# Expert results copied out of PSUM earlier in the next expert's second unit

## What is computed

```python
shared = jax.nn.silu(xt @ sw1) * (xt @ sw3) @ sw2
...
h = jax.nn.silu(jnp.einsum('td,edh->eth', xt, w1)) * jnp.einsum('td,edh->eth', xt, w3)
y = jnp.einsum('eth,ehd->etd', h, w2)
...
out = jnp.einsum('te,etd->td', comb, y) + shared
```

## Time and profile before

| what | value |
|---|---|
| median of 3 runs | 856.68 us (854.65 to 857.11) |
| the profiled execution | 855.59 us |
| its span in the trace | 854.0 us |
| granted TensorE clock, mean | 0.955 of full |
| TensorE busy | 767.4 us (90%) |
| VectorE busy | 554.9 us (65%) |
| ScalarE busy | 460.8 us (54%) |
| GpSimd busy | 301.0 us (35%) |

### The profile page before, as it was taken

One profiled execution on the slowest core, in us unless ns is written; L12 is line 12 of the kernel. 1 busy time (PEld: TensorE's weight loads), 2 busy tenths in 40 slices (PEclk: granted clock), 3 DMA queues, 4 the chain that ended last, 5 costly groups with the idle time before them and its releaser, 6 DMA issues. The chain is left out here.

```text
span 854.0 us, 13328 instructions
## 1 busy us (share of the span) xinstructions
PE 767.4 (90%) x4993; PEld 640.5 (75%) x4993; DVE 554.9 (65%) x904; ACT 460.8 (54%) x748; POOL 301.0 (35%) x189
## 2 busy tenths in 40 slices
PE   3997799999999978899996999799889899898894
PEld 2664588787878753899995999688788787786784
DVE  6628997979797926454226444478686786777755
ACT  4244596868686825633334332356565665566530
POOL 8240686868686820000000004033222222232333
PEclk9999799999999989899998699999999999999998
DMA  9320830000000006000004208756565766556015
GB/s 260 119 41 9 298 67 2 1 2 2 1 2 2 1 9 251 1 1 1 2 0 152 71 1 297 249 175 224 174 237 193 231 207 210 194 196 218 34 37 162
DMA packets 66460, 92.46 MB, mean 108 GB/s; under 512 B 6723, under 2 KB 44197, under 8 KB 65877
## 3 DMA queue, kind: packets, MB, share of 16 engines
q1 hardware_dynamic: 64149, 85.77, 30.9%
q0 software_dynamic: 2240, 5.76, 2.2%
HBM read 80.69 MB, written 10.82 MB: 107 GB/s over the span
## 5 line engine op out<-in xcount | busy, mean ns | idle before, releaser
L1581 POOL TENSOR_TENSOR w_lo<-weights_far,w_hi 128x1024 fp32r<-128x1024 f32 x32 | 77.0, 2406 | 210.9 <-ACT w_hi L1699 210.9
L660 POOL TENSOR_TENSOR bias_exp_hi<-edge_exp_hi,mask 128x640 fp32r<-128x640 f32 x40 | 98.0, 2451 | 71.3 <-PE ps L806 32.3
L1784 PE MATMUL ps<-xT,w_hi 128*128 128x480 f32 (+7 forms) x512 | 112.1, 342 | 3.6 <-DVE w_lo L1601 3.6
L1784 PEld LDWEIGHTS ps<-xT,w_hi 128*128 128x128 f32 x512 | 84.6, 194 | 9.9 <-issue 4.1
L1786 PEld LDWEIGHTS ps<-xT,w_lo 128*128 128x128 f32 x512 | 74.7, 192 | 1.7
L1786 PE MATMUL ps<-xT,w_lo 128*128 128x240 f32 (+7 forms) x512 | 75.4, 270 | 0.0
L806 PE MATMUL ps<-onehot,bias_exp_hi 128*128 128x314 f32 x400 | 69.5, 320 | 5.4 <-POOL bias_exp_hi L660 5.0
L1799 PE MATMUL ps<-w_hi,hidden_hi 128*128 128x512 f32 (+7 forms) x120 | 52.1, 434 | 23.0 <-DVE weights_near L1629 21.0
L1618 DVE TENSOR_TENSOR hT<-hT 128x240 f32<-128x240 f32 (+7 forms) x64 | 63.2, 988 | 11.3 <-ACT hT L1716 11.3
L1699 ACT ACTIVATE w_hi<-weights_far 128x1024 fp32r<-128x1024 f32 x64 | 67.1, 1050 | 0.0
L806 PE MATMUL ps<-onehot,bias_exp_lo 128*128 128x314 f32 x400 | 65.7, 311 | 0.0
(11 more groups left out here) (272 smaller groups left out, 1678.8 us busy)
## 6 DMA issues: line engine op xcount, KB each, us to landing
weights_far<-in_L_ffn_w SPq DMA_DIRECT2D x64, 512.0 KB, 5.5
weights_near<-in_L_ffn_w SPq DMA_DIRECT2D x32, 512.0 KB, 3.6
weights_near<-in_L_gnn_W SPq DMA_DIRECT2D x1, 4096.0 KB, 14.5
weights_near<-in_L_gnn_Wqkv SPq DMA_DIRECT2D x3, 1024.0 KB, 8.2
weights_ff<-in_L_gnn_W SPq DMA_DIRECT2D x1, 3072.0 KB, 13.9
weights_lo_shared<-in_L_ffn_sw SPq DMA_DIRECT2D x6, 512.0 KB, 7.7
weights_near<-in_L_ffn_sw SPq DMA_DIRECT2D x6, 512.0 KB, 6.7
slot_rows<-zeros SPq DMA_DIRECT2D x1, 2944.0 KB, 26.1
```

Of the source, the lines that this page charges most:

```text
L660: pool.tensor_tensor(to.rearrange("p t (h d) -> p t h d", h=H), e[:, b, :, :].unsqueeze(3).broadcast_to([P, CT, H, BN]), m.unsqueeze(2).br ...
L1581: pool.tensor_tensor(w2s[u][1], raw_rest[2] if v == V else raw[u][2], w2s[u][0], ALU.subtract)\
L1784: pe.matmul(both(bank, cap), w[u % 2][0][:, c, cut], xT(r)[:, c, :, :], start=c == 0, stop=False)
```

## The change

In VectorE's loop over the units, the call that copies the results of expert r - 1 is put between the first weight part of the unit and its first sum, instead of between the first product and the second sum. It is still in the second unit. Nothing else differs.

```diff
             for v in range(V):
                 r, u = v // UNITS, v % UNITS
                 weights_lo(v + 1, 0)
+                if u == 1 and r:
+                    results(r - 1)
                 parts_summed(v, 0)
                 weights_lo(v + 1, 1)
                 hidden(v, 0)
-                if u == 1 and r:
-                    results(r - 1)
                 parts_summed(v, 1)
                 if u == 2 and r + 1 < EX:
                     rows_lo(r + 1)
```

## The result

The changed kernel takes 844.69 us (median of 4 runs, 842.90 to 846.38), the kernel before beside it 856.89 us (854.65 to 857.95). The ratio is 0.9861, with a 95% interval of 0.9832 to 0.9889: 12.2 us faster, where 13.2 was forecast. The profiled execution has a span of 841.2 us, against 854.0.

A forecast was written before the change was run, and what follows sets the result against it. A dependency loop through ScalarE, VectorE and GpSimd sets the shortest unit, with TensorE late after pausing for copies. Savings of 13.9 us, less 0.1 per expert, give -13.2: 843.5 us for the median, range 841.0 to 850.0.

The forecast's parts named there:

- step 3: VectorE, second units: sum, GpSimd's pass and the held product come 1.20 us later behind the copies; seven times, 8.4 us.
- steps 1 and 2: TensorE's down-projection at 224: pause about 1.45 us instead of 3.42, then full clock, block 2.83 us instead of 4.39.
- t0: Start of a unit's first weight split on ScalarE, from which the forecast counts times within an expert.
- step 4: Third units: ScalarE's 3.23 us wait for TensorE goes, later waits too, and the unit reaches its shortest length.
- ring length: Shortest unit length, set by a dependency loop through ScalarE, VectorE and GpSimd: 7.85 us at capacity 224, then 7.75, 7.63.
- The sum: Whole program: the experts' savings together -13.9 us, less 0.1 per expert given back, so -13.2 us.
- the list: New and old lengths of experts by capacity, 224 to 128, second unit to next second unit; savings together -13.9 us.
- the allowance for the row splits: 0.1 us per expert given back, because the third unit also splits the next expert's rows.
- the first rival: TensorE's clock still falls behind the pauses: 0.6 us per expert, 4.2 in all, giving 847.7 us; chance 0.18.
- TensorE's new waits: TensorE's remaining waits for the copies: 1.45 us, then about 2.1, 2.4, 3.0; about 12 us in all, from 21.0.
- nothing: TensorE gains 8.7 us at its pauses, the 8.4 us price is paid in series: net -0.3, 856.4 us; chance 0.07.
- slower: Third unit's up-projections are held by something else, TensorE's early start is worth nothing: 8.4 us price, 865.1 us; chance 0.05.

The follow-up runs named there:

- two sizes of copies: Copies of experts 0 to 6 cut to 8 of 512 columns, in the changed kernel (ratio 0.9721) and in the kernel before (ratio 0.9920).
- short copies: The kernel before, with the copies of experts 0 to 6 cut to 8 of 512 columns: 852.89 us, ratio 0.9920.

## Why the prediction was right

**The step from 7.85 to 9.05 (step 3).** Right: 9.08, and +1.2 at every expert. The two sizes of copies showed that the price hangs on the place.

**The earlier start and the clock (steps 1 and 2).** Right at 224: a pause of 1.48 us for 1.45, a block of 2.86 for 2.83, the next up-projections 5.91 us after t0 (596.94 to 602.85) for 5.88 forecast. The step went from pause length to clock, and there it was too simple: the clock stayed full behind 2.27 and 2.64 us and fell behind 1.94 and 2.00.

**What it buys (step 4).** Right: ScalarE's wait fell from 25.0 to 0.6 us, and third units have ring length.

**The sum.** By expert, second unit to second unit (208, for instance, from 629.64 to 661.87): 32.70, 32.23, 31.64, 31.17, 31.31 and 30.21 us, where the list says 32.50, 32.08, 31.59, 31.08, 30.62 and 30.17. Five are within 0.2, the allowance for the row splits included in none of them. The sixth, capacity 160, is 0.7 long, and this is the first rival in small: behind the pause of 1.94 us the clock fell, and ScalarE then waited twice for TensorE, 0.27 and 0.30 us. The rival had put such a case at 0.6 us. It happened at one expert with consequences (at 128 the clock fell too, but TensorE has more room there), not at seven. The list alone comes to 13.9 us and the window shows 12.6. Of the 1.3 between them 0.7 is this one and 0.6 is spread over the others, about what the forecast gave back for the row splits (0.7). So what was off is the clock behind the pause at capacity 160, for which the sum had no term.

**TensorE's new waits.** 11.2 us for about 12; the one at 144 was 1.54 and not 2.4, as TensorE arrived later from the slow block before it (1.56 us more work in an expert that was 0.7 longer).

**The rivals "nothing" and "slower"** failed where the prediction said they would be decided. "Nothing" needed ScalarE's wait to stay, and it went. For "slower" the third unit's matmuls had to be held by a weight part; they started at 5.91 us after t0, right behind the block before them. The GPSIMD Engine Reference of the Trainium skill, Key points, says that GpSimd contends with Vector instructions that have two inputs in SBUF. The trace agrees: the product was held for 2.11 us beside the pass, and copies that no longer lie under the pass cost 1.2 us a time. That was not the whole sum.

What stays open is how the clock is decided. Pauses of equal length ended in either way (2.27 us: full in the second profile of the kernel before, low in the one with short copies), and no experiment here kept a pause and varied what TensorE does ahead of it.

## What to carry to other kernels

When an engine waits for an instruction that is ready long before its turn, ask what the turn costs in the place that it would move to: the same copies cost the unit 0 under another engine's pass, 1.2 us at the head of its ring, and almost 0 in a wait at the end of the unit before. Read a unit's shortest length off the units that nobody disturbs, and add to it; here that gave the time to 1.2 us. And when an engine's short instructions sometimes last five times as long, look at which engine's instruction ends just before they do: moving GpSimd's work onto the busier VectorE brought more (ratio 0.9594) than any place for the copies (0.9741).

## What the runs showed of the hardware that was not expected

- GpSimd's subtraction of 128 x 1024 and VectorE's instructions with two SBUF inputs held each other up, in both directions: a product of 0.38 us took 2.1 to 2.6, and a pass of 2.40 took 2.98 when it began in the middle of a weight part. Copies and sums that read PSUM were not held (1.28 and 0.61 us, with and without a pass beside them).
- TensorE's clock fell behind pauses of 1.94 us (changed kernel) and 2.00 us (copies behind the first sum), and stayed full behind one of 2.64 us (kernel before); the first and the last were the same in a second profile. With short copies in the kernel before it fell behind 2.27 and stayed full behind 2.50 and 2.72. Behind these pauses the first matmul still ran at full speed (0.47 us) and the fall came one to four matmuls later; in the first profile of the kernel before it was slow already behind 2.79 and 3.42 (0.76 us), and not behind 3.02 and 3.23.
- The same 9 matmuls without purpose in each pause, 2.25 us of extra work, made the kernel before 1.3% faster.
